# Two neighbouring banks per maximum instruction, and VectorE for seven of eight copies of the heads' bank

## The chip, the cores and the metric

The kernel runs on one core of a Trainium2 chip. The core has a matrix engine (TensorE, PE in the profile), a vector engine (VectorE, DVE), an activation engine (ScalarE, ACT), GpSimd (POOL) and a queue that issues DMAs (SyncE, SP). Matrix products land in PSUM, which the program treats as eight banks of 512 fp32 numbers in each of 128 partitions. The metric is the device time of one execution in microseconds. Before the change it is 3399.02 us, the median of three runs (3393.05 to 3400.91).

## The reference

For 16 batches of 1024 rows of 256 numbers:

```
x = x + layernorm(attention(layernorm(x)))     # on the left 128 columns, 16 heads of 8
x = x + layernorm(ffn(layernorm(x)))
attention: q, k, v = left @ W.T; softmax(q k^T / 4) over keys; out @ Wo.T + bo
ffn: 3 cycles of  h = gelu(h@w1+b1), gelu(h@w2+b2), gelu(h@w3+b3), sigmoid(h@w4+b4)
     out = out + coupling * twist(out)
```

The softmax needs, for each query row and head, the maximum over all 1024 keys. The kernel forms these maxima from products made for that purpose alone. They are subtracted inside the later score products, by three more rows of the queries (split in three bf16 parts), so that ScalarE's exponential needs no bias of its own.

## The kernel before

The program is written out engine by engine, each engine in its own loop over batches. Semaphores tie the engines together. A batch b passes an attention of 64 steps, and then a coupling of 30 beats, in which the network of batch b-1 runs beside the entry and exit work of other batches.

**A step of the attention.** One step handles four heads and one of eight blocks of keys. TensorE issues two score products (`scores`, line 499, first half), some maximum products (`max_unit`, line 481), two more score products, perhaps more maximum products, the weighing of the step before (`weigh`, line 514, eight passes in the trace), and a last maximum product. ScalarE does two exponentials over two banks each (`exp`, line 719). Eight steps make a group. At a group's end the bank `heads_ps` holds the weighted sums of four heads. ScalarE copies it to `headsT` (`take_heads`, line 728) after both exponentials of the next step, and the next group's first weighing waits for that copy through `heads_evac`.

**The maxima.** There are 256 units a batch. A unit is one product of 128 queries against 512 keys into one bank. VectorE reduces the bank to one column of `max_parts` (line 966). After 32 units a small VectorE instruction joins the two halves of the keys (`max_all`, line 972), GpSimd splits the result in three, and DMAs lay it as rows. Units of batch b+1 are worked on in the last part of batch b. In the attention of batch 0 a step has four units (1 after the first scores, 2 after the second scores, 1 after the weighing). In later attentions it has three (2, 0, 1).

**The ring.** `ring_bank` gives the bank whose last use is the oldest, and waits for the instruction that emptied it. In an attention there are three such banks, in a coupling five: the bank of the heads and one of the score banks join. Products other than maxima (transposes, projections) take banks of the same ring and count as two turns younger (`REST`). VectorE reads units strictly in their order, each as soon as `max_done` tells of it.

The number of units in a step or beat comes from these lines, and is not changed:

```python
return units_until(LEAD0 + 4 * n + (1, 3, 4)[third])                                # batch 0
return units_until(b * UNITS + LEAD + min(IN_ATTENTION, 3 * n + (2, 2, 3)[third]))  # later ones
```

The functions that the change touches follow.

Of the kernel before, what the change touches and what calls it, by code (L numbers as in the profile page):

```python
# [6 lines left out]
F32 = mybir.dt.float32  # L7
# [78 lines left out]
def attention_ffn_program(nc, a):  # L86
# [10 lines left out]
    with ExitStack() as ctx:  # L97
# [6 lines left out]
        scoresT_ps = ctx.enter_context(nc.psum_tensor("scoresT_ps", [P, 4 * BANK], F32))  # L104

        ring_ps = ctx.enter_context(nc.psum_tensor("ring_ps", [P, RING * BANK], F32))
        heads_ps = ctx.enter_context(nc.psum_tensor("heads_ps", [P, BANK], F32))
# [38 lines left out]
        max_parts = sb("max_parts", [P, 2, 2, MU])  # L146
# [100 lines left out]

        def laid(b):

            return 16 * (24 * (b // 2 + 1) - (12 if b % 2 == 0 else 0))  # L250
# [6 lines left out]
        banks = [ring_ps[:, i * BANK:(i + 1) * BANK] for i in range(RING)]  # L257
        banks += [scoresT_ps[:, FFN_BANKS * BANK:], heads_ps[:, :]]
# [3 lines left out]


# [4 lines left out]
        def layer_bank(b, l, second=0):  # L268
            i = FIRST_BANK[l] + second
            return banks[RING - 1 + i] if b == N - 1 else scoresT_ps[:, i * BANK:(i + 1) * BANK]  # L270

        def coupling_banks(l):
            i = FIRST_BANK[l]
# [172 lines left out]
        def tensor_program(e):  # L446
# [11 lines left out]
            def ring_bank(evacuated, count, rest=0):  # L458
                i = min(range(ring[0]), key=lambda k: turn[k])
# [15 lines left out]
            def max_unit(u):  # L475
# [5 lines left out]
                e.matmul(ring_bank(max_taken, u + 1),  # L481
# [3 lines left out]
            def scores(b, n, two):  # L485
# [11 lines left out]
                for side in range(2):  # L497
                    rows = slice(64 * side, 64 * side + ROWS + MROWS)
                    m = e.matmul(scoresT_ps[:, (2 - 2 * two + side) * BANK:(3 - 2 * two + side) * BANK],  # L499
# [212 lines left out]
        def scalar_program(e):  # L712
            def exp(b, n, two):
# [3 lines left out]
                if two == 0 and n == 0 and valid(b - 2):  # L717
                    e.wait_ge(ffn_done[0], BEATS * (b - 1))
                e.activation(p_sb[:, n % 2, 2 * two:2 * two + 2, :].rearrange("p h n -> p (h n)"),  # L719
                             scoresT_ps[:, (2 - 2 * two) * BANK:(4 - 2 * two) * BANK], ACT.Exp,  # L720
                             scale=SCALE).then_inc(exp_done, 1)

            def take_heads(b, n):
                group = n // NT
                e.wait_ge(pv_done, step_of(b, n) + 1)
# [167 lines left out]
            for b in range(-1, N):  # L893
                if b == 0:
                    e.wait_ge(const_dve, 2)
                for n in range(STEPS):
# [3 lines left out]
                    if valid(b) and n and n % NT == 0:  # L900
                        take_heads(b, n - 1)
                if valid(b):
                    take_heads(b, STEPS - 1)
# [49 lines left out]
        def vector_program(e):  # L953
            def max_units(done, upto):
                for u in range(done, upto):
                    if u < N * UNITS:
                        max_unit(u)
# [527 lines left out]
```

## Time and profile before

| | |
|---|---|
| median of three runs | 3399.02 us |
| all three | 3399.02, 3400.91, 3393.05 us |
| span of the profiled execution, first to last instruction | 3391.6 us |
| mean granted clock of TensorE | 0.985 of full |
| busy: TensorE, VectorE, ScalarE | 3222.9, 2992.7, 2843.6 us |
| TensorE waiting (weight loads) for VectorE's maxima, total over 2131 waits | 1242.4 us |
| maximum reductions on VectorE | 4096 of about 0.68 us |

The profiled execution's time with what lies outside the span is not recorded by itself. The span is 1.5 to 9.3 us below the three runs. In the profile PEld is the loading of weights, which overlaps the products, so that an idle time of PEld is not yet one of TensorE. The "idle before" of an engine names what ended the idle time.

### The profile page before, as it was taken

What the parts mean: (1) busy time and instruction counts of PE and PEld (TensorE: products, weight loads), DVE (VectorE), ACT (ScalarE), POOL (GpSimd) and SP (SyncE); (2) the same over time, 40 slices, a digit from 0 to 9 for tenths busy, and PEclk for the clock granted to TensorE, in tenths of its full rate; (3) what the DMA queues carried; (4) which work ended last, traced back from release to release, by engine and by line L of the source; (5) the groups of instructions that cost most, each with busy time, mean ns of one, the idle gap of its engine ahead of it and who ended that gap; (6) DMA issues with size and microseconds to landing.
All of it is one profiled execution on the core that took longest, in us unless ns stands there. A gap on an engine that the chain in (4) does not pass through costs nothing.

```text
span 3391.6 us, 56526 instructions
## 1 busy us (share of the span) xinstructions
PE 3222.9 (95%) x19712; PEld 941.5 (28%) x19712; DVE 2992.7 (88%) x5577; ACT 2843.6 (84%) x3752; POOL 897.6 (26%) x1322
## 2 busy tenths in 40 slices
PE   6989999999999999999999999999999999999987
PEld 2222232322323232232322323232232322323223
DVE  7999989999898998989989898998989989898943
ACT  3868979798897979979798897979979798896975
POOL 5002050321505123050320505123050320504015
PEclk7998999999999999999999999999999999999999
DMA  3111111121111112121121111112121121111001
GB/s 90 26 41 43 32 50 33 44 50 44 50 31 51 43 39 55 33 61 32 44 49 44 50 31 51 42 39 55 33 61 32 45 49 44 38 32 51 8 22 38
DMA packets 97498, 144.75 MB, mean 43 GB/s; under 512 B 49472, under 2 KB 60096, under 8 KB 89408
## 3 DMA queue, kind: packets, MB, share of 16 engines
q1 hardware_dynamic: 93520, 123.83, 13.8%
q0 software_dynamic: 3696, 17.31, 2.8%
q8 instruction: 158, 2.59, 0.3%
q14 instruction: 124, 1.02, 0.1%
HBM read 34.61 MB, written 32.51 MB: 20 GB/s over the span
## 4 chain that ended last, share of the span: by engine, by line
PE 67%; DVE 17%; ACT 8%; issue 3%; SPq 2%; DMA 1%; POOL 1%; DVEq 0%; POOLq 0%; ACTq 0%
PE heads_ps L514 24%; PE ring_ps L481 15%; DVE max_parts L966 12%; PE scoresT_ps L499 11%; PE scoresT_ps L602 7%; ACT p_sb L719 4%; DVE stats L977 3%; PE scoresT_ps L607 2%; ACT headsT L728 1%; PE ring_ps L543 1%; SPq L346 1%; DVE state L1030 1%; ACT state L784 1%; DVE moments L987 1%; PE ring_ps L529 1%
## 5 line engine op out<-in xcount | busy, mean ns | idle before, releaser
L966 DVE TENSOR_REDUCE max_parts<-ring_ps 128x1 f32<-128x512 f32 x3744 | 2369.2, 683 | 225.4 <-PE ring_ps L481 166.3
L719 ACT ACTIVATE p_sb<-scoresT_ps 128x1024 f32<-128x1024 f32 x2048 | 1970.1, 1024 | 81.4 <-PE scoresT_ps L499 57.7
L481 PE MATMUL ring_ps<-k_rows,q_rows 48*128 48x512 bf16 x3744 | 1086.0, 384 | 33.1 <-DVE max_parts L966 23.8
L514 PE MATMUL heads_ps<-p_sb,v_sb 128*9 128x512 f32 x8192 | 1071.4, 595 | 17.9 <-ACT headsT L728 11.9
L499 PE MATMUL scoresT_ps<-q_rows,k_rows 51*128 51x512 bf16 x4096 | 1021.3, 383 | 7.1 <-ACT p_sb L719 4.3
L481 PEld LDWEIGHTS ring_ps<-k_rows,q_rows 48*128 48x128 bf16 x3744 | 265.5, 94 | 1353.4 <-DVE max_parts L966 1242.4
L1233 POOL CAST max_wide<-max_all 128x16 bf16<-128x16 f32 x128 | 25.4, 198 | 1743.0 <-DVE max_all L972 1743.0
L602 PE MATMUL scoresT_ps<-state,w 128*128 128x512 f32 x732 | 364.9, 621 | 13.3 <-DVE state L1030 12.3
L824 ACT ACTIVATE p_sb<-scoresT_ps,b 128x512 f32<-128x512 f32 x180 | 123.8, 688 | 194.2 <-PE scoresT_ps L602 193.2
L499 PEld LDWEIGHTS scoresT_ps<-q_rows,k_rows 51*128 51x128 bf16 x4096 | 207.0, 93 | 224.4 <-ACT p_sb L719 211.5
L514 PEld LDWEIGHTS heads_ps<-p_sb,v_sb 128*9 128x9 f32 x8192 | 124.4, 88 | 288.8 <-issue 278.3
L607 PE MATMUL scoresT_ps<-p_sb,w 128*128 128x512 f32 x360 | 178.5, 618 | 0.1
L966 DVE TENSOR_REDUCE max_parts<-heads_ps 128x1 f32<-128x512 f32 x225 | 153.2, 681 | 24.0 <-PE heads_ps L481 23.2
L602 PEld LDWEIGHTS scoresT_ps<-state,w 128*128 128x128 f32 x732 | 125.6, 191 | 158.0 <-issue 151.4
L732 ACT ACTIVATE x_in<-x_in,offset,rstd 128x128 f32<-128x128 f32 (+1 forms) x248 | 119.9, 537 | 38.3 <-POOL offset L1243 38.3
L826 ACT ACTIVATE p_sb<-scoresT_ps,b 128x512 f32<-128x512 f32 x90 | 61.3, 681 | 76.8 <-PE scoresT_ps L607 76.8
L1241 POOL TENSOR_TENSOR rstd<-rstd,minus_half 128x8 f32<-128x8 f32 x63 | 111.3, 1767 | 5.2
L977 DVE BATCH_NORM_STATS2 stats<-x_in 128x6 f32<-128x256 f32 x248 | 90.9, 410 | 13.2 <-ACT x_in L792 9.8
L1240 POOL TENSOR_SCALAR rstd<-moments 128x8 f32<-128x8 f32 x63 | 15.9, 253 | 321.1 <-DVE moments L987 319.5
L1285 POOL TENSOR_TENSOR couple<-couple,state 128x512 f32<-128x512 f32 x60 | 76.5, 1275 | 71.8 <-ACT couple L815 71.8
L1294 POOL TENSOR_TENSOR state<-state,couple 128x512 f32<-128x512 f32 x60 | 77.8, 1297 | 64.8 <-DVE couple L1021 63.4
L966 DVE TENSOR_REDUCE max_parts<-scoresT_ps 128x1 f32<-128x512 f32 x127 | 86.2, 678 | 8.5 <-PE scoresT_ps L481 8.4
(196 smaller groups left out, 2635.9 us busy)
## 6 DMA issues: line engine op xcount, KB each, us to landing
q_rows<-parts SPq DMA_DIRECT2D x744, 32.0 KB
k_rows<-parts SPq DMA_DIRECT2D x744, 32.0 KB
x_sb<-in_x SPq DMA_DIRECT2D x16, 1024.0 KB, 4.8
x_in<-in_x SPq DMA_DIRECT2D x15, 1024.0 KB, 5.4
out<-x_sb SPq DMA_DIRECT2D x15, 1024.0 KB, 3.9
out<-x_in POOLq DMA_DIRECT2D x15, 1024.0 KB, 7.9
q_rows<-max_rows SPq DMA_DIRECT2D x512, 3.0 KB
feat_h<-headsT SPq DMA_DIRECT2D x512, 16.0 KB
```

What stands on the lines that cost most here:

```text
L481: e.matmul(ring_bank(max_taken, u + 1), q_rows[rows, slot, pair, h * BANK + qb * P:h * BANK + (qb + 1) * P], k_rows[rows, slot, pair, kh * ...
L499: m = e.matmul(scoresT_ps[:, (2 - 2 * two + side) * BANK:(3 - 2 * two + side) * BANK], k_rows[rows, slot, pair, kb * P:(kb + 1) * P], q_ro ...
L514: m = e.matmul(heads_ps[32 * j:32 * j + DH + 1, :], v_sb[:, b % 2, kb, 4 * (group % NG) + j, 0:DH + 1], p_sb[:, n % 2, j, :], start=(kb == ...
L602: o = e.matmul(ps, w1[:, f, m * P:(m + 1) * P], state[:, b % 2, f, c * BANK:(c + 1) * BANK], start=(f == 0), stop=(f == 1))
L607: o = e.matmul(ps, w2[:, f, :], hidden[k][:, 0, 2 * c + f, :], start=(f == 0), stop=(f == 1))
L719: e.activation(p_sb[:, n % 2, 2 * two:2 * two + 2, :].rearrange("p h n -> p (h n)"), scoresT_ps[:, (2 - 2 * two) * BANK:(4 - 2 * two) * BA ...
L732: m = e.activation(dst(t), src(t), ACT.Identity, bias=offset[i][:, t:t + 1], scale=rstd[i][:, t:t + 1])
L824: e.activation(hidden[k][:, 0, 2 * c + m, :], ps, ACT.Gelu, bias=b1[:, m:m + 1]).then_inc(hid_done[k], 1)
L966: e.tensor_reduce(max_parts[:, gi % 2, kh, col:col + 1], bank_of(max_taken, u + 1), AX.X, ALU.max).then_inc(max_taken, 1)
L977: m = e.bn_stats(stats[i][:, t, :], src(t))
L1241: finished(e.tensor_tensor(rstd[i][:, :], rstd[i][:, :], minus_half[:, :], ALU.pow))
L1294: e.tensor_tensor(half, half, couples[k][:, 2, :], ALU.add).then_inc(state_a_done[k], 1)
```

## The change

1. PSUM becomes one tensor, `all_ps`: banks 0 to 2 are the ring, 3 the heads, 4 to 7 the scores. The score banks swap their order, so that the one lent to the ring in a coupling (bank 4) lies beside the heads' bank. The coupling's layers keep to the other three.
2. TensorE's `max_units` looks, before each unit that is not the last of its stretch, for two neighbouring banks among the three oldest of the ring (`oldest_pair`). If there are two, this unit and the next take them, and VectorE reduces both with one instruction of 1024 elements that writes two columns. Both banks then wait for that one instruction to end. `max_parts` is laid out by unit, and the join reads it through a pattern.
3. VectorE copies the heads' bank in seven of eight groups (`take_heads`), between the second and the third stretch of units in the group's next step. ScalarE keeps the last copy of a batch, after its last exponential.

```diff
-                for u in range(done, upto):
-                    if u < N * UNITS:
-                        max_unit(u)
+                u, upto = done, min(upto, N * UNITS)
+                while u < upto:
+                    pair = oldest_pair() if u + 1 < upto else ()
+                    size = 2 if pair else 1
+                    first_of.append(u)
+                    for v in range(u, u + size):
+                        taken_by[v] = len(first_of)
+                        max_unit(v, pair[v - u:v - u + 1])
+                    u += size
+
+            def oldest_pair():
+                oldest = sorted(range(ring[0]), key=lambda k: turn[k])[:3]
+                pairs = [(i, j) for i, j in itertools.permutations(oldest, 2) if starts[j] - starts[i] == BANK]
+                return min(pairs, key=lambda ij: max(turn[ij[0]], turn[ij[1]])) if pairs else ()
...
-                e.tensor_reduce(max_parts[:, gi % 2, kh, col:col + 1], bank_of(max_taken, u + 1),
-                                AX.X, ALU.max).then_inc(max_taken, 1)
+                e.tensor_reduce(out, units_banks(u, size), AX.X, ALU.max).then_inc(max_taken, 1)
...
-                e.activation(headsT[:, group // NG, group % NG, :], heads_ps[:, :], ACT.Copy).then_inc(heads_evac, 1)
+                e.tensor_copy(headsT[:, group // NG, group % NG, :], heads_ps[:, :]).then_inc(heads_evac, 1)
...
                 for n in range(STEPS):
+                    upto = units_in_step(b, n, 1)
+                    max_units(done, upto)
+                    done = max(done, upto)
+                    if valid(b) and n and n % NT == 0:
+                        take_heads(b, n // NT - 1)
                     upto = units_in_step(b, n, 2)
```

In the whole program the order of VectorE after the change has 1393 reductions of two banks, 1310 of one, and 112 copies of the heads' bank. By place: 64 of two and 128 of one in the attention of batch 0, 64 and 64 in each later attention that has maxima throughout, about 24 and 15 in each full coupling.

VectorE in the attention of batch 0, before: units one by one, and a join after 32 of them.

```order
L966 TENSOR_REDUCE max_parts<-heads_ps 128x1
L966 TENSOR_REDUCE max_parts<-ring_ps 128x1 x6
L972 TENSOR_TENSOR max_all<-max_parts 128x16
L966 TENSOR_REDUCE max_parts<-ring_ps 128x1 x32
L972 TENSOR_TENSOR max_all<-max_parts 128x16
```

The same place after, across the end of a group of steps (128x2 is a reduction of two banks).

```order
L997 TENSOR_REDUCE max_parts<-all_ps 128x1 x2
L997 TENSOR_REDUCE max_parts<-all_ps 128x2
L1006 COPY headsT<-all_ps 128x512
L997 TENSOR_REDUCE max_parts<-all_ps 128x1
L1014 TENSOR_TENSOR max_all<-max_parts 128x16
L997 TENSOR_REDUCE max_parts<-all_ps 128x1
L997 TENSOR_REDUCE max_parts<-all_ps 128x2
```

Two of a step's four units share an instruction, and the copy stands between the shared one and the next single one.

ScalarE from the end of a coupling into the attention of batch 1, before.

```order
L771 ACTIVATE v_sb<-ring_ps 128x64x8
L784 ACTIVATE state,sums<-ring_ps 128x512
L719 ACTIVATE p_sb<-scoresT_ps 128x1024 x18
L728 ACTIVATE headsT<-heads_ps 128x512
L719 ACTIVATE p_sb<-scoresT_ps 128x1024 x16
```

And after.

```order
L801 ACTIVATE v_sb<-all_ps 128x64x8
L814 ACTIVATE state,sums<-all_ps 128x512
L749 ACTIVATE p_sb<-all_ps 128x1024 x128
L758 ACTIVATE headsT<-all_ps 128x512
L854 ACT_TABLE_LOAD
```

The 128 exponentials of a batch are no longer broken by copies, and the last copy stays where it was.

VectorE at the start of the attention of batch 1, before.

```order
L966 TENSOR_REDUCE max_parts<-scoresT_ps 128x1
L966 TENSOR_REDUCE max_parts<-ring_ps 128x1 x26
L972 TENSOR_TENSOR max_all<-max_parts 128x16
L966 TENSOR_REDUCE max_parts<-ring_ps 128x1 x32
L972 TENSOR_TENSOR max_all<-max_parts 128x16
```

And after, at the end of its first group of steps.

```order
L1014 TENSOR_TENSOR max_all<-max_parts 128x16
L997 TENSOR_REDUCE max_parts<-all_ps 128x1
L997 TENSOR_REDUCE max_parts<-all_ps 128x2
L997 TENSOR_REDUCE max_parts<-all_ps 128x1
L997 TENSOR_REDUCE max_parts<-all_ps 128x2
L1006 COPY headsT<-all_ps 128x512
L997 TENSOR_REDUCE max_parts<-all_ps 128x1
L997 TENSOR_REDUCE max_parts<-all_ps 128x2
```

A step of three units is now one reduction of two banks and one of one bank. TensorE's own order of products is the same as before.

## Rows read from the trace of the kernel before

**Rows 1.** The page: busy us (share of the span) and instructions of each engine.

```profile
PE 3222.9 (95%) x19712; PEld 941.5 (28%) x19712; DVE 2992.7 (88%) x5577; ACT 2843.6 (84%) x3752; POOL 897.6 (26%) x1322
```

**Rows 2.** Busy us by stretch: batch 0's attention and coupling, a later pair, its middle.

```profile
74.00:232.60 158.60, 148.86 (x1009) 33.37 (x1009) 156.26 (x260) 127.41 (x136) 7.91 (x34) 0.99 0.12 26
232.60:287.10 54.50, 39.11 (x128) 15.48 (x127) 47.36 (x110) 22.81 (x51) 23.12 (x32) 0.69 0.22 71
1508.30:1637.30 129.00, 127.43 (x949) 27.14 (x949) 121.03 (x199) 125.63 (x137) 12.90 (x31) 1.00 0.17 40
1637.30:1711.80 74.50, 70.50 (x283) 30.87 (x283) 63.71 (x148) 52.57 (x102) 41.99 (x50) 1.00 0.20 52
1657.40:1692.50 35.10, 31.98 (x121) 12.95 (x120) 34.27 (x90) 25.88 (x48) 24.12 (x28) 1.00 0.08 32
```

**Rows 3.** Timeline, ScalarE, a later attention: start us, us, engine, line, operation.

```profile
1590.71 0.60 ACT L728 ACTIVATE headsT<-heads_ps 128x512 f32<-128x512 f32 x1
...
1606.85 0.60 ACT L728 ACTIVATE headsT<-heads_ps 128x512 f32<-128x512 f32 x1
```

**Rows 4.** The chain that ended last, same place: start us, us, what.

```profile
1593.60 0.97 PE heads_ps L514 x8
...
1605.49 0.97 PE heads_ps L514 x8
```

**Rows 5.** Timeline, TensorE, one step of the same attention.

```profile
1602.43 0.39 PE L481 MATMUL ring_ps<-k_rows,q_rows 48*128 48x512 bf16 x1
...
1602.67 0.59 PE L481 MATMUL ring_ps<-k_rows,q_rows 48*128 48x512 bf16 x2
...
1603.05 0.10 PEld L499 LDWEIGHTS scoresT_ps<-q_rows,k_rows 51*128 51x128 bf16 x2 [0.17 <-ACT p_sb L719]
...
1604.38 0.39 PE L481 MATMUL ring_ps<-k_rows,q_rows 48*128 48x512 bf16 x1
...
1604.80 0.09 PEld L481 LDWEIGHTS ring_ps<-k_rows,q_rows 48*128 48x128 bf16 x1 [0.30 <-DVE max_parts L966]
```

**Rows 6.** Timeline, VectorE: durations and distances of its instructions.

```profile
1604.06 0.68 DVE L966 TENSOR_REDUCE max_parts<-ring_ps 128x1 f32<-128x512 f32 x1
...
1604.81 0.69 DVE L966 TENSOR_REDUCE max_parts<-ring_ps 128x1 f32<-128x512 f32 x1
...
1605.53 0.17 DVE L972 TENSOR_TENSOR max_all<-max_parts 128x16 f32<-128x16 f32 x1
...
1656.84 0.69 DVE L1059 TENSOR_TENSOR y_sb<-scoresT_ps,bo 128x512 f32<-128x512 f32 x1 [0.17 <-PE scoresT_ps L543]
1657.45 1.39 DVE L977 BATCH_NORM_STATS2 stats<-y_sb 128x6 f32<-128x256 f32 x4
...
1676.08 0.68 DVE L966 TENSOR_REDUCE max_parts<-scoresT_ps 128x1 f32<-128x512 f32 x1
1676.68 0.68 DVE L966 TENSOR_REDUCE max_parts<-ring_ps 128x1 f32<-128x512 f32 x1
```

**Rows 7.** Timeline, batch 0's attention: ScalarE over eight steps, then one step.

```profile
96.54 1.94 ACT L719 ACTIVATE p_sb<-scoresT_ps 128x1024 f32<-128x1024 f32 x2
...
116.41 1.94 ACT L719 ACTIVATE p_sb<-scoresT_ps 128x1024 f32<-128x1024 f32 x2
...
151.01 0.69 DVE L966 TENSOR_REDUCE max_parts<-ring_ps 128x1 f32<-128x512 f32 x1
...
151.75 0.39 PE L481 MATMUL ring_ps<-k_rows,q_rows 48*128 48x512 bf16 x1
...
153.05 0.39 PE L481 MATMUL ring_ps<-k_rows,q_rows 48*128 48x512 bf16 x1
...
153.47 0.69 DVE L966 TENSOR_REDUCE max_parts<-ring_ps 128x1 f32<-128x512 f32 x1
```

**Rows 8.** Timeline, first beat of a coupling: TensorE and ScalarE.

```profile
1641.78 0.39 PE L481 MATMUL ring_ps<-k_rows,q_rows 48*128 48x512 bf16 x1 [0.57 <-DVE max_parts L966]
...
1640.98 0.25 ACT L798 ACTIVATE hg<-ring_ps,gb 128x1 f32<-128x1 f32 x1
```

More of the change, by code:

```diff
@@ L246, in step_of, with pack_of @@
             return b * STEPS + n
+        first_of, taken_by = [], {}
+        def pack_of(u):
+            first = first_of[taken_by[u] - 1]
+            return first, 2 if taken_by.get(first + 1) == taken_by[u] else 1
         def laid(b):
@@ L256, in attention_ffn_program, with units_banks @@
         place = {}
-        banks = [ring_ps[:, i * BANK:(i + 1) * BANK] for i in range(RING)]
-        banks += [scoresT_ps[:, FFN_BANKS * BANK:], heads_ps[:, :]]
+        starts = [i * BANK for i in (*range(RING), RING + 1, RING)]
+        banks = [all_ps[:, at:at + BANK] for at in starts]
         def bank_of(evacuated, count):
             return banks[place[evacuated.name, count]]
+        def units_banks(u, size):
+            ends = [starts[unit_bank[v]] for v in (u, u + size - 1)]
+            both = all_ps[:, min(ends):max(ends) + BANK].rearrange("p (k n) -> p k n", n=BANK)
+            return both[:, ::-1, :] if ends[0] > ends[1] else both
+        unit_bank = {}
         def track(b):
@@ L269, in layer_bank @@
             i = FIRST_BANK[l] + second
-            return banks[RING - 1 + i] if b == N - 1 else scoresT_ps[:, i * BANK:(i + 1) * BANK]
+            if b == N - 1:
+                return banks[RING - 1 + i]
+            at = FFN_BANKS - FIRST_BANK[l] - (1 - second if LAYERS[l][0] == 4 else 0)
+            return scoresT_ps[:, at * BANK:(at + 1) * BANK]
         def coupling_banks(l):
-            i = FIRST_BANK[l]
+            i = FFN_BANKS - FIRST_BANK[l] - 1
             return scoresT_ps[:, i * BANK:(i + 2) * BANK].rearrange("p (s n) -> p s n", s=2)[:, :, 0:HALF]
@@ L456, in spare_banks, with ring_bank @@
                         turn[i], freed[i] = next(turns), last
-            def ring_bank(evacuated, count, rest=0):
-                i = min(range(ring[0]), key=lambda k: turn[k])
+            def ring_bank(evacuated, count, rest=0, i=None):
+                if i is None:
+                    i = min(range(ring[0]), key=lambda k: turn[k])
                 if freed[i]:
@@ L498, in scores @@
                     rows = slice(64 * side, 64 * side + ROWS + MROWS)
-                    m = e.matmul(scoresT_ps[:, (2 - 2 * two + side) * BANK:(3 - 2 * two + side) * BANK],
+                    m = e.matmul(scoresT_ps[:, (2 * two + side) * BANK:(2 * two + side + 1) * BANK],
                                  k_rows[rows, slot, pair, kb * P:(kb + 1) * P],
@@ L954, in max_units @@
             def max_units(done, upto):
[L955 to L973 removed]
+                u = done
@@ new lines, in max_units, with max_pack @@
+                while u < min(upto, N * UNITS):
+                    first, size = pack_of(u)
+                    max_pack(first, size)
+                    u = first + size
+            def max_pack(u, size):
+                for v in range(u, u + size):
+                    gi = v // PER_GROUP
+                    e.wait_ge(max_done[v % 2], v // 2 + 1)
+                    if v % PER_GROUP == 0 and gi >= 2:
+                        e.wait_ge(max_joined, gi - 1)
+                at, last = u % (2 * PER_GROUP), (u + size - 1) % (2 * PER_GROUP)
+                out = max_parts[:, last:at + 1][:, ::last - at] if last < at else max_parts[:, at:last + 1]
+                e.tensor_reduce(out, units_banks(u, size), AX.X, ALU.max).then_inc(max_taken, 1)
+                for v in range(u, u + size):
+                    if (v + 1) % PER_GROUP == 0:
+                        join(v // PER_GROUP)
```

53 lines of the change are left out of this document (27 added, 26 removed).

## The prediction, on record before the changed kernel ran

> **What bounds the kernel now.** I first read the busy shares [rows 1]: TensorE 95%, VectorE 88%, ScalarE 84%. No engine is simply full, so I went to the stretches [rows 2], which show four different limits.
>
> In a later attention (129.0 us, fifteen of them) TensorE is busy 127.4, ScalarE 125.6 and VectorE 121.0. The chain of waits has weighings from 1593.60 to 1605.49, six steps in 11.89 us, so a plain step takes 1.98 us [rows 4]. Two copies of the heads' bank by ScalarE are 16.14 us apart [rows 3]. Eight plain steps are 15.85, so a group's end costs 0.29. Within a step, TensorE's third score product waits for ScalarE's exponential [rows 5]. A maximum's weight load waits 0.30 for VectorE there, but the product itself follows the one before it at the array's own distance of 0.21 (two products of 0.38 in 0.59), so it would not start earlier without the wait. So the step is a loop between TensorE and ScalarE, and VectorE only fits in.
>
> In the attention of batch 0 (158.6 us) VectorE is busy 156.3. Eight steps take 19.87 us, 2.48 each [rows 7]. I can close the loop: a unit's reduction at 151.01 frees the bank of the unit whose product starts at 151.75 (0.74 later); the single unit behind the weighing starts at 153.05 (1.30 later); its reduction starts at 153.47 (0.42 later). Sum 2.46: that reuse is the step.
>
> In a later coupling (74.5 us) TensorE is busy 70.5, but its middle, 35.1 us long, has VectorE at 34.3 [rows 2]: there VectorE's throughput sets the pace. The coupling of batch 0 has VectorE at 47.4 of 54.5.
>
> **Prices.** Back to back, single reductions start 0.60 apart and last 0.68 [rows 6]. The reduction of two banks is not in the trace. Four BN_STATS of 256 elements last 1.39 together; each adds about 0.33, against 0.60 for 512, so 256 elements cost 0.27 and the second 512 about 0.54 (my estimate from these rows). I take 1.14 us from start to start and 1.22 duration. That saves 0.06 of a pair's 1.20. The ends: 1.20 (nothing saved) and 1.08 (twice the saving). VectorE's copy of 512 elements out of PSUM has its nearest row in the addition of the bias, 0.69 long and 0.61 to the next start [rows 6]; I take 0.60 and 0.68, with 0.48 and 0.69 as the ends. From a reduction's end to the weight load that it frees is 0.06 (1604.06 + 0.68 to 1604.80) [rows 5, 6].
>
> The Trainium skill ("VectorE: DVE Perf Modes", the section on the TRN2 errata) gives a VectorE instruction that reads PSUM 120 cycles plus one per element at 0.96 GHz. That would be 0.66 us for one bank, close to the 0.68 duration in [rows 6], and it would save 0.125 us for each pair rather than 0.06. The 0.60 from start to start speaks against the full 120 cycles, since part of them overlaps the next instruction. By the page the stretches where VectorE is full would gain twice as much (a rival below).
>
> **Batch 0's attention: pairs.** The ring has banks 0, 1, 2. A step takes a single unit, a pair, a single unit. Say a pair has 1 and 2. Then the singles take 0 and 1, and the next pair must be two neighbours of {2, 0, 1}: it becomes 0 and 1. Bank 1 is that of the unit just before. In the following step the singles take 2 and 0, and the pair 1 and 2, whose last user lies one unit further back. So in every second step, 32 times, TensorE's pair waits for the newest reduction. Its loop is the 2.46 from above plus the one single reduction between the two, 0.60: 3.06 us, against 2.46. The price of the pair's own reduction is not on that path. Cost 32 x 0.60 = +19.2 us. From the other side: it is 0 if something else covers it, but VectorE has no other work there.
>
> **Batch 0's attention: copies.** VectorE's copy starts after the pair's reduction, 0.42 + 1.14 = 1.56 after the pair's product; the single unit behind the weighing would start at 1.30 + 0.42 = 1.72; with the copy it starts at 2.16. Seven copies at 0.44: +3.1. ScalarE's copies cost nothing there: eight steps with one inside take 19.87 - 8 x 2.46 = 0.19 more, about the join of 0.17 [rows 6, 7]. Bounds 0 and 7 x 0.6 = 4.2.
>
> **Later attentions.** Three banks, and pair, single, pair, single always take (1,2), 0, (1,2), 0. Here VectorE's loop runs: single product to its reduction 0.43 (1604.38 to 1604.81), to the pair's 0.60, until both banks are free 1.22 + 0.06, and from the second product of a pair (1602.88, as the x2 row ends at 1603.26) to the next single product 1.50 (1604.38) [rows 5, 6]. Sum 3.81 for two steps, against 3.96. It fits with 0.15 to spare, so the plain step stays 1.98. At a group's end the copy enters: 0.43 + 0.60 + 1.14 (pair, then copy) + 0.60 (copy) + 0.60 (single) + 1.28 (pair freed) + 1.50 = 6.15 for three steps of 5.94. So the copy on VectorE costs 0.20, where ScalarE's costs 0.29. What goes on ScalarE comes back, for the most part, as a late release of the pair. Gain 0.09 x 7 x 15 = -9.5. The weighing of the new group needs the copy by about 2.97 after that single product and has it at 2.17 + 0.68 + 0.06 = 2.91, just in time. Two of six joins in an attention stand behind a single unit, and their 0.17 or a little more uses up the 0.15: I put 0.05 on each, +1.5. Together -8.0. The ends: -30.5 if the copy is free (0.29 x 105), and +6 if the copy is 0.1 longer in effect and joins cost their full 0.17.
>
> **Couplings.** In the middle of each of 14 full couplings are 9 or 10 pairs: -0.6. In the first beat five units come at once while a small product holds one of five banks. Before, the fifth unit waited 0.57 for a reduction, until 1641.78. Now the pair search leaves it the bank that ScalarE frees at 1640.98 + 0.25, so that it can go about 0.45 earlier [rows 8]: -0.45. Against that, a pair chosen for being neighbours is less old than the oldest: about five packs in a coupling take a bank of the pack just before them. Each could cost up to 0.5 (release 0.06, product 0.39, its signal 0.04) if VectorE had nothing in between; mostly it has statistics or an update there. I take +0.4 together, between 0 and 2.5. Net -0.65 x 14 = -9. The two couplings before batch 1's attention have 48 pairs, mostly where VectorE is full: -2.
>
> **Sum.** +19.2 + 3.1 - 8.0 - 9 - 2 = +3.3 us. Against the profiled span that is 3391.6 + 3.3 = 3394.9, and with the same distance to the median as before, 3399.0 + 3.3 = 3402. VectorE's busy time falls by about 1393 x 0.14 (two durations of 0.68 become one of 1.22) and rises by 112 x 0.68: 2992.7 - 195 + 76 = about 2875. ScalarE's falls by 112 x 0.60 = 67.
>
> **Rivals.**
> - *The copy leaves ScalarE for nothing* (faster). For it: VectorE has 8 us idle in a later attention, and 0.15 to spare per two steps. It decides if a pair's banks are free earlier than I think, or the copy is 0.48. Then -30.5 in the attentions, no stalls in the couplings (-15), -3 in the first ones, with batch 0's +22: -26. Time 3373.
> - *A pair's late release stalls TensorE in the couplings* (slower). For it: TensorE works in order, and its layer products stand behind the waiting unit. Against: in the middle VectorE is behind anyway. It decides from about three fully exposed stalls in a coupling. With four, +2.0 - 1.05 = +0.95 each, x 14 = +13, and 22.3 - 8.0 - 2 for the rest: +25. Time 3424.
> - *Batch 0's pair wait is hidden*: without the +19.2, 3383.
> - *The fixed part of an instruction is saved in full*: another 0.06 on some 135 pairs in the couplings and 48 before: -11. Time 3391. The page cited above is the rule behind it.
>
> **Chances.** Forecast 0.40, with its own range 3391 to 3413; copy for nothing 0.24; stalls 0.22; hidden wait 0.08; full saving 0.06. A difference under 0.2% (6.8 us) can't be told from none. The forecast's case gives 0.05 faster, 0.22 same, 0.13 slower; the stalls are all slower; the copy for nothing and the hidden wait are faster but for 0.01; the last is split 0.04 and 0.02. Faster 0.40, same 0.25, slower 0.35. The range runs from 3373, where the copy costs nothing, to 3428, a little past four stalls a coupling.
>
> **What would show it.** Batch 0's attention 181 us long rather than 158.6, with steps alternating between about 3.1 and 2.5. Later attentions at 128.5, each group's end near 0.2 long, the plain step still 1.98. The pair's reduction near 1.22. Couplings at 73.9. If batch 0's attention is not longer, the ring argument is wrong. If the plain step moves, VectorE's loop was not the loose one. If couplings are longer than 74.5, the stalls are real.

## The result and the profile after

The changed kernel takes 3442.8 us (median of four runs, 3439.8 to 3446.0). The kernel before takes 3398.6 in the same comparison. The ratio is 1.0135, with a 95% interval of 1.012 to 1.0149: slower by 44 us, where 3 were forecast and 3428 was the upper end. One run of a later version (no pairs in the last three beats of a coupling) took 5073 us at a mean granted clock of 0.554 and is left out of its figures.

The page after shows the engine shares, the chain by engine, and the group of the maximum reductions. These answer to [rows 1].

```profile
PE 3229.5 (94%) x19712; PEld 933.8 (27%) x19712; DVE 2981.0 (87%) x4296; ACT 2809.0 (82%) x3640; POOL 893.3 (26%) x1322
...
PE 58%; DVE 26%; issue 6%; SPq 5%; ACT 2%; DMA 2%; POOL 1%; DVEq 0%; POOLq 0%
...
L997 DVE TENSOR_REDUCE max_parts<-all_ps 128x2 f32<-128x1024 f32 (+1 forms) x2703 | 2492.9, 959 | 322.7 <-PE all_ps L511 277.1
```

VectorE is busy 12 us less, yet its share of the chain that ended last rose from 17% to 26%. It has less to do and is waited for more (the chain before, on its page):

```profile
PE 67%; DVE 17%; ACT 8%; issue 3%; SPq 2%; DMA 1%; POOL 1%; DVEq 0%; POOLq 0%; ACTq 0%
```

Next, the groups of VectorE with shapes kept apart (count, then busy us and mean ns of one, then the idle time before them).

```profile
L997 DVE TENSOR_REDUCE max_parts<-all_ps 128x2 f32<-128x1024 f32 x1393 | 1687.1, 1215 | 131.4 <-PE all_ps L511 128.4 <-issue 1.2
L997 DVE TENSOR_REDUCE max_parts<-all_ps 128x1 f32<-128x512 f32 x1310 | 893.6, 687 | 191.3 <-PE all_ps L511 148.6 <-DVE max_all L1014 0.5
...
L1006 DVE COPY headsT<-all_ps 128x512 f32<-128x512 f32 x112 | 76.2, 681 | 15.2 <-PE all_ps L544 15.2
```

The prices were right: the pair lasts 1.215 us (1.22 forecast), the copy 0.681 (0.68).

The stretches after, in the order of [rows 2]: the attention of batch 0, the coupling behind it, a later attention, a later coupling. The columns are start:end and length, then busy time (and count) of PE, PEld, DVE, ACT, POOL, then the granted clock, DMA share and GB/s.

```profile
77.00:262.10 185.10, 167.96 (x1007) 31.57 (x1008) 161.88 (x205) 123.84 (x129) 7.82 (x34) 0.95 0.10 23
262.10:322.10 60.00, 40.55 (x135) 16.40 (x127) 46.94 (x90) 23.43 (x50) 23.06 (x32) 0.61 0.22 68
1552.20:1681.00 128.80, 126.78 (x949) 26.30 (x946) 120.91 (x142) 123.38 (x130) 12.17 (x31) 1.00 0.16 38
1681.00:1756.80 75.80, 70.32 (x283) 31.17 (x285) 62.65 (x123) 52.45 (x100) 41.94 (x50) 1.00 0.20 53
```

VectorE had 2.3 us idle in batch 0's attention before, and has 23 now.

I divided both profiled executions at ScalarE's exponentials, and set the differences of all stretches against the forecast's terms. An attention reaches from the first start to the last end of its 128 exponentials, and a coupling fills the time between two attentions. The differences add up to the 51.1 us between the two spans. That is 7 more than between the medians: the span before lies only 1.5 us under the fastest of its four runs. So some microseconds of the table may be spread between executions.

| part | forecast | measured |
|---|---|---|
| prologue | (in -2) | +3.0 |
| batch 0's attention | +22.3 | +26.5 |
| coupling before batch 1 | -2 | +5.6 |
| attention of batch 1 | (in -8.0) | +2.4 |
| 14 later couplings | -9 | +17.0 |
| 14 later attentions | -8.0 | -3.7 |
| tail | 0 | +0.4 |

Two rows are far off: the couplings by 26 us, and the early stretches around the first coupling by 13.

**The clock.** The granted clock in the early stretches was this in the kernel before:

```profile
237.50:278.40 40.90, 28.21 (x71) 11.13 (x71) 35.38 (x87) 14.29 (x29) 18.15 (x28) 0.58 0.20 66
```

And after:

```profile
268.40:278.60 10.20, 3.62 (x8) 2.52 (x8) 7.93 (x18) 1.85 (x5) 3.47 (x8) 0.50 0.55 160
285.50:329.90 44.40, 35.87 (x113) 12.37 (x117) 32.72 (x57) 23.94 (x45) 19.59 (x24) 0.50 0.17 56
```

Of the 40.9 us before, 34.2 are at half (1.2 GHz of 2.4). After there are 54.6, and the last 8 of them lie in the attention of batch 1, where TensorE sets the pace. The forecast had no term for the clock in these stretches.

In batch 0's attention the clock also dips, which means here that it is granted at half for some 3.4 us and then at full again. The first row is a whole group of eight steps, from one copy of the heads' bank to the next, with such a dip in it (the third row). The second is a group without. The fourth is the dip in the last group.

```profile
102.05:126.08 24.03, 21.94 (x131) 4.08 (x128) 20.66 (x28) 15.50 (x16) 0.83 (x4) 0.93 0.10 22
172.90:195.75 22.85, 20.61 (x131) 3.84 (x128) 20.61 (x28) 15.50 (x16) 0.83 (x4) 1.00 0.11 24
104.60:108.00 3.40, 3.40 (x16) 0.58 (x16) 2.25 (x3) 0.60 (x1) 0.07 (x1) 0.50 0.16 34
...
244.60:248.00 3.40, 3.40 (x20) 0.76 (x16) 2.72 (x4) 1.73 (x2) 0.00 (x0) 0.51 0.18 39
```

A dip of 3.4 us costs that group 1.18 us. Three groups have one (the second, the third and the last), and in the first group the clock is at half for 6.8 us.

**The couplings.** At the end of a later coupling TensorE projects the values into a bank of the ring, and works in order. Before (start us, us, engine, line; in brackets the idle time before it, shown where it is large):

```profile
1708.50 1.29 DVE L966 TENSOR_REDUCE max_parts<-ring_ps 128x1 f32<-128x512 f32 x2 [0.38 <-PE ring_ps L481]
...
1709.25 0.60 PE L535 MATMUL ring_ps<-wv,feat_x 128*128 128x128 f32 x3
```

After, the same place:

```profile
1753.58 1.82 DVE L997 TENSOR_REDUCE max_parts<-all_ps 128x2 f32<-128x1024 f32 x2 [0.58 <-PE all_ps L511]
...
1754.86 0.60 PE L565 MATMUL all_ps<-wv,feat_x 128*128 128x128 f32 x3 [0.77 <-DVE max_parts L997]
```

Before, the projection starts 0.75 us after the first of two reductions began: that one lasts 0.69, and the release takes 0.06. After, it starts 1.28 after the pair's reduction began: 1.22 and 0.06. It wanted one bank and had to wait for two.

The projection isn't the only place. I compared the two kernels product by product in the coupling behind batch 12's attention (three other couplings give the same figures within 0.03). The columns are the time into the coupling before, TensorE's wait there before and after, and how far the changed kernel is behind once that place is passed.

| place | product | wait before | wait after | behind |
|---|---|---|---|---|
| 4.5 | fifth maximum of the first beat | 0.57 | 0.08 | -0.48 |
| 21.7 | a maximum | 0.00 | 0.67 | -0.05 |
| 27.1 | a maximum | 0.00 | 0.27 | +0.22 |
| 38.8 | a maximum | 0.18 | 0.51 | +0.55, back to +0.34 by 60 |
| 62.6 | a maximum | 0.00 | 0.56 | +0.89 |
| 71.9 | projection of the values | 0.13 | 0.77 | +1.67, and +1.34 at the end |

The place at 62.6, before:

```profile
2717.38 0.38 PE L481 MATMUL heads_ps<-k_rows,q_rows 48*128 48x512 bf16 x1
```

And after:

```profile
2768.19 0.39 PE L511 MATMUL all_ps<-k_rows,q_rows 48*128 48x512 bf16 x2 [0.56 <-DVE max_parts L997]
```

So about half a microsecond of a coupling's loss arises at a maximum, and 0.44 of the projection's 0.64 reaches the end.

### The profile page after: what moved, and what is told of

It is laid out like the page before. It is cut to its first block, busy times and chain, and to the rows that moved or that the text cites. A ratio compares the mean times of both kernels' runs of the same rounds, so it can differ in the third digit from the quotient of the medians.

```text
span 3442.7 us, 56452 instructions
## 1 busy us (share of the span) xinstructions
PE 3229.5 (94%) x19712; PEld 933.8 (27%) x19712; DVE 2981.0 (87%) x4296; ACT 2809.0 (82%) x3640; POOL 893.3 (26%) x1322
## 4 chain that ended last, share of the span: by engine, by line
PE 58%; DVE 26%; issue 6%; SPq 5%; ACT 2%; DMA 2%; POOL 1%; DVEq 0%; POOLq 0%
DVE max_parts L997 19%; PE all_ps L544 19%; PE all_ps L511 14%; PE all_ps L529 8%; PE all_ps L632 7%; SPq L362 3%; PE all_ps L637 3%; DVE stats L1019 3%; PE all_ps L573 2%; DVE headsT L1006 2%; SPq L337 1%; PE all_ps L559 1%; ACT p_sb L749 1%; PE all_ps L565 1%; DMA max_rows<-max_wide 1%
## 5 line engine op out<-in xcount | busy, mean ns | idle before, releaser
L997 DVE TENSOR_REDUCE max_parts<-all_ps 128x2 f32<-128x1024 f32 (+1 forms) x2703 | 2492.9, 959 | 322.7 <-PE all_ps L511 277.1
L749 ACT ACTIVATE p_sb<-all_ps 128x1024 f32<-128x1024 f32 x2048 | 1974.2, 1021 | 144.8 <-PE all_ps L529 105.1
L511 PE MATMUL all_ps<-k_rows,q_rows 48*128 48x512 bf16 x4096 | 1108.8, 391 | 104.0 <-DVE max_parts L997 82.3
L544 PE MATMUL all_ps<-p_sb,v_sb 128*9 128x512 f32 x8192 | 1074.8, 597 | 7.3 <-ACT p_sb L749 4.9
L529 PE MATMUL all_ps<-q_rows,k_rows 51*128 51x512 bf16 x4096 | 1032.5, 384 | 3.4 <-ACT p_sb L749 2.3
L511 PEld LDWEIGHTS all_ps<-k_rows,q_rows 48*128 48x128 bf16 x4096 | 256.9, 93 | 1503.2 <-DVE max_parts L997 1242.0
L632 PE MATMUL all_ps<-state,w 128*128 128x512 f32 x768 | 382.6, 622 | 8.4 <-DVE state L1072 6.0
L854 ACT ACTIVATE p_sb<-all_ps,b 128x512 f32<-128x512 f32 x180 | 123.7, 687 | 193.0 <-PE all_ps L632 192.5
L529 PEld LDWEIGHTS all_ps<-q_rows,k_rows 51*128 51x128 bf16 x4096 | 208.4, 93 | 199.8 <-ACT p_sb L749 188.4
L637 PE MATMUL all_ps<-p_sb,w 128*128 128x512 f32 x360 | 178.5, 618 | 0.1
L856 ACT ACTIVATE p_sb<-all_ps,b 128x512 f32<-128x512 f32 x90 | 61.3, 681 | 79.7 <-PE all_ps L637 79.7
L1341 POOL TENSOR_TENSOR state<-state,couple 128x512 f32<-128x512 f32 x60 | 77.6, 1294 | 54.5 <-DVE couple L1063 53.1
L1006 DVE COPY headsT<-all_ps 128x512 f32<-128x512 f32 x112 | 76.2, 681 | 15.2 <-PE all_ps L544 15.2
```

The costliest lines, as they stand in the source:

```text
L511: e.matmul(ps, q_rows[rows, slot, pair, h * BANK + qb * P:h * BANK + (qb + 1) * P], k_rows[rows, slot, pair, kh * BANK:(kh + 1) * BANK], s ...
L529: m = e.matmul(scoresT_ps[:, (2 * two + side) * BANK:(2 * two + side + 1) * BANK], k_rows[rows, slot, pair, kb * P:(kb + 1) * P], q_rows[r ...
L544: m = e.matmul(heads_ps[32 * j:32 * j + DH + 1, :], v_sb[:, b % 2, kb, 4 * (group % NG) + j, 0:DH + 1], p_sb[:, n % 2, j, :], start=(kb == ...
L632: o = e.matmul(ps, w1[:, f, m * P:(m + 1) * P], state[:, b % 2, f, c * BANK:(c + 1) * BANK], start=(f == 0), stop=(f == 1))
L637: o = e.matmul(ps, w2[:, f, :], hidden[k][:, 0, 2 * c + f, :], start=(f == 0), stop=(f == 1))
L854: e.activation(hidden[k][:, 0, 2 * c + m, :], ps, ACT.Gelu, bias=b1[:, m:m + 1]).then_inc(hid_done[k], 1)
```

## The experiments

### Pairs taken out, copies kept

```diff
-                    pair = oldest_pair() if u + 1 < upto else ()
+                    pair = oldest_pair() if u + 1 < upto and False else ()
```

> The changed kernel with every maximum reduced by itself and banks taken oldest first; VectorE still makes the copies. Ring theory (a pair takes a bank whose last reader stands just ahead, and frees both late): batch 0's attention falls from 185.2 to about 161 (158.6 plus a little for seven copies on VectorE), the couplings from 75.8 to 74.5, later attentions 129.2, since single reductions leave VectorE less room for the copy; time about 3400. Rival (the copies on VectorE are what costs): batch 0's attention stays above 170 and the time above 3425.

Measured: 3410.1 us, ratio 1.0032 (1.0023 to 1.0042). Its stretches, batch 0's attention and a later coupling:

```profile
74.60:237.30 162.70, 149.16 (x1009) 33.30 (x1009) 159.90 (x267) 123.87 (x129) 7.90 (x34) 0.99 0.11 26
1849.80:1924.30 74.50, 70.56 (x283) 30.88 (x283) 63.95 (x148) 52.62 (x102) 42.02 (x50) 1.00 0.20 52
```

The full couplings are those of before, so all of their loss comes from the pairs. A later attention takes 129.62: without pairs VectorE's copies cost 0.6 each attention, and 4.1 in batch 0.

### Copies back on ScalarE, pairs kept

```diff
-                    if valid(b) and n and n % NT == 0:
-                        take_heads(b, n // NT - 1)
```

This goes from VectorE's loop, and the lines removed from ScalarE's come back.

> The changed kernel with all copies of the heads' bank back on ScalarE; pairs as changed. Ring theory: batch 0's attention about 182 (3 us less), couplings unchanged at 75.8, later attentions about 129.0 (0.2 more); time about 3443, the same as the changed kernel. Rival (copies on VectorE cost): time below 3425.

Measured: 3446.4 us, ratio 1.0132 (1.0114 to 1.015). Batch 0's attention:

```profile
75.60:253.10 177.50, 163.48 (x1008) 30.70 (x1008) 158.21 (x198) 127.42 (x136) 7.87 (x34) 0.99 0.11 24
```

Pairs alone cost 18.9 us there, against the 19.2 forecast. A group of eight steps is 22.35 long (copies by ScalarE on the chain of time, two of them):

```profile
144.39 0.60 ACT L758 ACTIVATE headsT<-all_ps 128x512 f32<-128x512 f32 x1
166.74 0.60 ACT L758 ACTIVATE headsT<-all_ps 128x512 f32<-128x512 f32 x1
```

With VectorE's copy and a full clock it is 22.85 (above). So the copy costs 0.50 each, 3.5 for seven, near the forecast's 0.44 and 3.1. The other 4.2 us of the difference of 7.7 go with the clock. The changed kernel has four dips of 3.4 us more in this stretch (one in each of three groups, and 6.8 rather than 3.4 us in its first group), and 4 x 1.18 = 4.7.

### Batch 0 one by one

```diff
+                    pair = oldest_pair() if u + 1 < upto and stage != ["step", 0] else ()
```

`stage` holds the kind of stretch, its batch, and where needed the number of the step or beat that TensorE's program is written for.

> The changed kernel with no pairs in the attention of batch 0 alone. Ring theory: that attention falls by about 23 us to 162, nothing else moves by more than 1 us: time about 3420. Rival (VectorE as such is too full there, whoever is paired): falls by less than 5 us.

Measured: 3417.4 us, ratio 1.0051 (1.0036 to 1.0066). Batch 0's attention is 162.4. The coupling behind it also fell, from 60.0 to 55.2, though the pairs in it are unchanged. The coupling has 30.7 us at half clock and the attention behind it 3.4, together as much as before. This looks as if the slow attention had passed the loss on, but the next experiment speaks against so simple an account.

### Pairs in the later attentions only

```diff
+                    pair = oldest_pair() if u + 1 < upto and stage[0] == "step" and stage[1] > 0 else ()
```

> The changed kernel with pairs only in the attentions of batches 1 to 15, none in batch 0's attention or in any coupling. Ring theory: batch 0's attention 162, couplings 74.4 each (0.4 less if the wait in their first beat goes by the new order of banks, as there it did with pairs), first couplings back at 74.0 and 54.4, later attentions 128.8: time about 3392, near the kernel before or a little under it. Rival (the couplings lose by the new layout or by what VectorE leaves over from the attention): couplings stay at 75.8 and the time at about 3412.

Measured: 3406.3 us, ratio 1.0022 (1.001 to 1.0033). The couplings are back at 74.47, as expected, but not the time. Five attentions in a row (batches 5 to 9) took 130.2 to 130.6 rather than 128.7, each with a dip of the clock. The last experiment below turns on them.

Batch 0's attention is 162.4, and neither it nor the coupling behind it has a pair. Even so that coupling is not back at 54.5:

```profile
237.40:295.10 57.70, 42.72 (x127) 16.60 (x126) 47.70 (x110) 23.21 (x50) 23.20 (x32) 0.63 0.22 71
```

It has 43.2 us at half clock, and 8.0 follow in the attention of batch 1. Over the profiled executions this coupling goes with its time at half clock, whatever the pairs: 53.1 us with 27.3 at half (no pairs), 54.4 with 34.1 (before), 57.7 with 43.2 (here), 60.0 with 46.9 (changed). What keeps the clock at half for so long is not shown.

### The same banks, read one by one

This tells apart what the choice of the banks costs and what the common instruction costs. Each bank has an instruction of its own, the choice is that of the change.

```diff
-                    first_of.append(u)
                     for v in range(u, u + size):
+                        first_of.append(v)
                         taken_by[v] = len(first_of)
```

> The banks are chosen exactly as in the changed kernel, neighbours among the three oldest, but each bank is reduced and given back by an instruction of its own. Theory 1 (one instruction for two banks needs both products and returns both banks together, so that VectorE idles while TensorE fills them): without it VectorE is busy through, batch 0's attention falls back from 185.2 us to about 162.7 (the 162.7 without pairs), full couplings from 75.8 to 74.5, the whole to about 3411. Theory 2 (taking a bank that is not the oldest costs by itself): the banks are the same, so batch 0's attention stays over 175 us and couplings near 75.5, the whole about 3435.

Measured: 3457.4 us, ratio 1.0171 (1.0158 to 1.0184). Batch 0's attention, and a later coupling (five are like it; six have a dip of the clock and take 76.2 to 77.0; one takes 75.7 without one):

```profile
77.00:262.60 185.60, 158.66 (x1008) 33.28 (x1008) 161.97 (x268) 123.81 (x128) 7.75 (x33) 0.95 0.10 22
862.60:937.20 74.60, 71.02 (x286) 31.16 (x286) 63.65 (x149) 52.69 (x103) 41.92 (x50) 1.00 0.20 52
```

Each theory is right in one place. In batch 0 the choice alone does all the damage (185.6, my expectation of 162.7 fell). In the couplings without a dip the choice costs 0.1 and the common instruction the other 1.2: product by product, the maximum at 62.6 and the projection lose nothing here. The whole is still slower than the changed kernel. The later attentions take 129.6 rather than 128.8, and ten dips stand in couplings and attentions where the changed kernel has none. Two steps of batch 0 in this run, TensorE:

```profile
152.86 0.39 PE L511 MATMUL all_ps<-k_rows,q_rows 48*128 48x512 bf16 x1
...
154.04 0.39 PE L511 MATMUL all_ps<-k_rows,q_rows 48*128 48x512 bf16 x1 [0.35 <-DVE max_parts L997]
154.63 0.39 PE L511 MATMUL all_ps<-k_rows,q_rows 48*128 48x512 bf16 x1 [0.21 <-DVE max_parts L997]
...
155.93 0.39 PE L511 MATMUL all_ps<-k_rows,q_rows 48*128 48x512 bf16 x1
...
158.40 0.39 PE L511 MATMUL all_ps<-k_rows,q_rows 48*128 48x512 bf16 x1
```

And VectorE:

```profile
153.29 2.49 DVE L997 TENSOR_REDUCE max_parts<-all_ps 128x1 f32<-128x512 f32 x4 [0.37 <-PE all_ps L511]
156.35 2.48 DVE L997 TENSOR_REDUCE max_parts<-all_ps 128x1 f32<-128x512 f32 x4 [0.58 <-PE all_ps L511]
```

The steps are 3.07 and 2.47 long, the forecast's 3.06 and 2.46. In the long one TensorE's second and third maxima wait for reductions of the step itself, the weighing stands behind them, and VectorE then has 0.58 with nothing to read. With three banks, one reused a place too early is enough.

### Pairs only where the two oldest banks are neighbours

```diff
-                oldest = sorted(range(ring[0]), key=lambda k: turn[k])[:3]
+                oldest = sorted(range(ring[0]), key=lambda k: turn[k])[:2]
```

> A pair is formed only where the two oldest banks are neighbours: 155 pairs in the full couplings rather than 337, of which 16 (before 71) take a bank of the pack just before them; 43 rather than 64 pairs in batch 0's attention, none but one with the newest bank; the later attentions keep theirs. Theory 1a (what costs is a pair on a bank of the pack just before): batch 0's attention about 163 us, full couplings about 74.7, the whole about 3400 to 3405. Theory 1b (each pair costs by its joint release, however old its banks are): batch 0's attention about 175 (43/64 of the extra), couplings about 75.1, the whole about 3425.

Measured: 3424.2 us, ratio 1.0072 (1.0059 to 1.0085). Batch 0's attention and a later coupling, then the projection of the values in it.

```profile
74.70:237.00 162.30, 151.87 (x1009) 29.72 (x1009) 160.31 (x226) 123.87 (x129) 7.81 (x34) 0.99 0.12 26
1654.90:1730.40 75.50, 70.11 (x283) 30.79 (x283) 63.23 (x138) 53.13 (x102) 42.20 (x50) 1.00 0.20 53
```

And TensorE's row:

```profile
1728.19 0.49 PE L565 MATMUL all_ps<-wv,feat_x 128*128 128x128 f32 x2 [0.87 <-DVE max_parts L997]
```

Again one theory holds in each place. In batch 0 the 43 pairs with the oldest banks cost nothing. In the couplings 155 pairs rather than 337, and 16 rather than 71 that take a bank of the instruction just before, still cost 1.08 of the 1.34 us. So neither how young a pair's banks are nor how many pairs there are explains the loss. It comes in the same two places as in the changed kernel: product by product, a coupling is 0.13 behind until the maximum at 62.6, 0.67 after it, and then the projection waits 0.74 us longer than before.

### No pairs in the last three beats of a coupling

```diff
+                    pair = oldest_pair() if u + 1 < upto and not (
+                        stage[0] == "beat" and stage[1] > 0 and stage[2] >= BEATS - 3) else ()
```

> As the changed kernel, but no pair in the last three beats of the full couplings. In the changed kernel's trace the projection of the values takes a bank of the pair just before it and waits 0.77 us for its one instruction, where before it waited 0.13 for the first of two. Theory (TensorE's other products wait for the joint release): the wait is back at 0.13 and full couplings fall from 75.8 to 75.15, the whole to about 3434. Rival (the loss is spread, and a later wait takes its place): couplings within 0.2 of 75.8, the whole about 3442.

Measured: 3440.1 us (three runs), ratio 1.0129 (1.0111 to 1.0147). A coupling, and then TensorE's row of the projection in another:

```profile
2086.50:2161.80 75.30, 70.49 (x283) 31.06 (x283) 63.30 (x126) 52.63 (x102) 41.95 (x50) 1.00 0.20 52
```

```profile
1749.72 0.49 PE L566 MATMUL all_ps<-wv,feat_x 128*128 128x128 f32 x2
```

The wait of 0.77 is gone (0.14 is left), and the coupling is 0.44 shorter, of the 0.64 expected. The maximum at 62.6 still waits 0.56. The whole time can't be told from the changed kernel's: 1.0129 against 1.0135, with intervals that overlap. Five attentions now have a dip of the clock that the changed kernel did not have (1.6 to 1.9 us each), and they give back the 5 us won.

### Pairs in the attentions and in the first beat

```diff
+                    pair = oldest_pair() if u + 1 < upto and (
+                        stage[1] > 0 and (stage[0] == "step" or stage[2] == 0)) else ()
```

> Pairs in the attentions of batches 1 to 15 and in the first beat of the couplings only (five units at once), nowhere in batch 0. As forecast: the first beat's gain of 0.45 is kept, full couplings 74.0. Rival (the middle, where VectorE is full, swallows it, since VectorE's work is the same): 74.4 to 74.5 as with no pairs. Batch 0's attention 162.4 either way, the whole 3398 to 3408.

Measured: 3415.1 us, ratio 1.0059 (1.0038 to 1.008). Both expectations missed: couplings of 75.1, and five of them with a dip take 76.7 to 77.0. The first beat's fifth unit:

```profile
1852.59 0.61 PE L512 MATMUL all_ps<-k_rows,q_rows 48*128 48x512 bf16 x4
1854.40 0.39 PE L512 MATMUL all_ps<-k_rows,q_rows 48*128 48x512 bf16 x1 [1.20 <-DVE max_parts L1000]
```

Here the ring comes into the coupling in another order, the fifth unit gets a bank of a pair, and waits 1.20, where it waited 0.57 before and 0.08 in the changed kernel. The gain that I had forecast for this beat hangs on which bank comes up, not on the pair search as such.

### Layout alone

Every maximum by itself and all copies on ScalarE, on the new places of the banks and with the new `max_parts` (both edits above together).

> The new places of the banks and the new max_parts alone: every maximum by an instruction of its own, all copies on ScalarE. If layout and join cost nothing: 3398, batch 0's attention 158.6, later attentions 129.0, couplings 74.45. The difference to the version with single maxima and VectorE's copies (162.7 and 129.6) is then the copies' own price without pairs: 4.1 in batch 0 and 0.6 for each later attention. Rival: the join through a pattern costs some 0.1 us more each, 0.6 for each attention; then 3406 and the copies are free.

Measured: 3398.9 us, ratio 1.0000 (0.9991 to 1.0009), later attentions 129.07, couplings 74.47. The layout and the join's pattern cost nothing that can be told from none. The prologue has 47.8 us at half clock here as in the changed kernel (37.5 before) and is 75.1 long rather than 74.0, so about 1 of the 3.0 us in the table needs no pair.

### Each stage as it does best, and the start of an attention

Pairs in the later attentions only, copies by ScalarE in batch 0 and by VectorE later:

```diff
-                    if valid(b) and n and n % NT == 0:
+                    if valid(b) and b and n and n % NT == 0:
                         take_heads(b, n // NT - 1)
```

ScalarE's own copy stands where it stood before, for batch 0 alone.

> Pairs only in the attentions of batches 1 to 15, copies by VectorE there, by ScalarE in batch 0; couplings and batch 0 one by one. From the phases of the earlier runs: batch 0's attention 158.6 as before, couplings 74.5, later attentions 128.8: 15 x 0.25 = 3.8 gained. If the granted clock stays full in the attentions of batches 5 to 9, about 3394; if it halves for some us at the start of each of them as in the run with the same pairs (five times 1.5 us), about 3402. A rival: the changed order of the banks in the prologue costs by itself, then above 3402.

Measured: 3404.5 us (3394.6 to 3415.0, twelve runs), ratio 1.0016 (1.0005 to 1.0027). Then the same with pairs from the third step on:

```diff
+                    pair = oldest_pair() if u + 1 < upto and (
+                        stage[0] == "step" and stage[1] > 0 and stage[2] >= 2) else ()
```

> As the version with pairs in the later attentions only and ScalarE's copies in batch 0, but pairs begin with the third step of each attention. In that version TensorE waited 0.88 us in the first three of an attention and the granted clock then fell to half for 3.4 us in eight of fifteen attentions, 1.6 us longer each. Theory (these waits bring the clock down): without them no such stretches, later attentions 128.7, the whole about 3394. Rival (the clock falls for another reason, such as the whole attention's pattern): some attentions still 130.2, the whole 3400 to 3405.

Measured: 3390.5 us (3387.2 to 3393.0), ratio 0.9979 (0.9969 to 0.9988), faster than both kernels. TensorE at the start of an attention in the first of the two:

```profile
1512.74 0.39 PE L512 MATMUL all_ps<-k_rows,q_rows 48*128 48x512 bf16 x1 [0.18 <-ACT state L822]
...
1513.66 0.39 PE L530 MATMUL all_ps<-q_rows,k_rows 51*128 51x512 bf16 x2 [0.22 <-ACT p_sb L752]
1514.52 0.39 PE L512 MATMUL all_ps<-k_rows,q_rows 48*128 48x512 bf16 x2 [0.47 <-DVE max_parts L1007]
```

The stretches that follow:

```profile
1512.60:1514.80 2.20, 1.36 (x10) 0.45 (x10) 1.77 (x3) 2.20 (x4) 2.20 (x3) 1.00 0.37 75
1514.80:1518.20 3.40, 3.40 (x18) 0.56 (x15) 1.98 (x3) 1.67 (x3) 3.24 (x4) 0.51 0.77 248
1518.20:1530.00 11.80, 11.80 (x91) 2.43 (x88) 10.74 (x14) 11.39 (x12) 3.17 (x6) 1.00 0.16 49
```

With pairs from the third step:

```profile
1505.90:1508.20 2.30, 1.86 (x11) 0.59 (x10) 2.30 (x5) 2.30 (x5) 2.30 (x3) 1.00 0.57 116
1508.20:1511.60 3.40, 3.40 (x29) 0.70 (x28) 2.79 (x4) 3.24 (x4) 3.24 (x4) 1.00 0.72 239
1505.90:1634.40 128.50, 127.24 (x950) 26.60 (x949) 120.81 (x144) 123.36 (x130) 12.93 (x31) 1.00 0.17 40
```

The first version idles TensorE for 0.84 of 2.20 us, and does 18 products in the next 3.4 us, against 29. Eight of fifteen of its attentions (batches 7 to 14) have such a dip, the second version's one. A dip costs 1.6 us, and an attention without one is 128.66 in the first, 128.48 in the second. The first version's runs range over 20 us (with mean granted clocks from 0.974 to 0.981) and the second's over 6. So leaving the pairs out of the first two steps takes most of the dips away, and this is shown. That the length of the waits decides is not. The same three waits stand at the start of this version's attentions of batches 3 to 6, which have no dip, and of twelve attentions of the version with pairs in the first beat, of which one has a dip. And in the changed kernel TensorE idles for longer there, 1.26 us in one piece in the attentions of batches 2 to 14, and the clock stays full in all of them:

```profile
1553.76 0.39 PE L511 MATMUL all_ps<-k_rows,q_rows 48*128 48x512 bf16 x1 [1.26 <-DVE max_parts L997]
```

```profile
1552.20:1554.50 2.30, 1.04 (x10) 0.33 (x7) 1.82 (x3) 2.00 (x5) 2.22 (x4) 1.00 0.37 53
1554.50:1557.90 3.40, 3.40 (x28) 0.65 (x26) 3.28 (x4) 3.40 (x4) 3.32 (x3) 1.00 0.75 302
```

## Why the prediction was wrong

The step that failed is the stalls in the couplings, "+0.4 together, between 0 and 2.5". Three mistakes lie in it. I counted the pairs with young banks and priced those, but with hardly any of them left a coupling still loses 1.08. I looked only for maxima that wait, and TensorE's other products want a pair's banks too: the projection of the values waits 0.64 longer, of which 0.44 reaches the coupling's end. And I took most of the waits to be covered by VectorE's other work, while one maximum alone (at 62.6) costs half a microsecond. The gain of 0.45 set against them did come (a wait of 0.08 in place of 0.57), yet it was lost again after 22 of the 75 us, at a maximum that now waits 0.67. Net +1.2 a coupling (+1.34 in a plain one) in place of -0.65. The rival of stalls in the couplings was the right mechanism. Its own price of 3424 was short by 4 us in the couplings and mainly by the early stretches, which it had at -2 too.

The other terms, in order:

- *Batch 0's pairs, +19.2.* Right: 18.9, with steps of 3.07 and 2.47. The reason given, the choice of banks and not the common instruction, is shown by the same banks read one by one.
- *Batch 0's copies, +3.1.* 3.5 for the copies; the dips of the clock add some 4 that no term had.
- *The first two couplings, -2.* Wrong in sign: +3.0 and +5.6, and +2.4 more in the attention of batch 1. The first goes with 10 us more at half clock, the other two with about 20. With batch 0 one by one 4.8 of the 5.6 are gone, but with single maxima in the couplings as well 3.3 of them are back, so their cause stays open.
- *Later attentions, -8.0.* -0.25 each in the changed kernel, 3.7 in all. A group of eight steps with VectorE's copy takes 16.03 us in place of 16.14, 0.11 less where 0.09 was forecast, and two of seven take 16.27. The table shows why the two edits belong together there (an attention in us, full clock):

| | one by one | pairs |
|---|---|---|
| copies by ScalarE | 129.07 | 129.05 |
| copies by VectorE | 129.62 | 128.77 |
| the same, no pairs in the couplings | | 128.66 |
| the same, pairs from the third step | | 128.48 |

  Neither edit gains alone. Together they gain 0.3, and 0.55 where the couplings and the first two steps are left as they were: 15 x 0.55 = 8.2, near the forecast's 8.0. What I missed is the start of the attention, where the ring comes over from the coupling: TensorE waits there 1.26 us in one piece in the changed kernel, 0.43 in all before.
- *Prices.* From a pair's start to the next reduction's is 1.14 us (the row at 1753.58: 1.82 for both, less 0.68), as estimated. A pair saves 0.06 of 1.20. The rival of the full saving (0.12) has nothing for it.
- *VectorE busy 2875.* 2981. I subtracted durations (0.14 a pair), but a stretch counts overlapping instructions once, so that a pair saves 0.06 and a copy adds 0.60: 2992.7 - 84 + 67 = 2976.

The range failed with the stalls and the early stretches. Its upper end allowed four stalls of 0.5 us and nothing for the clock.

## What to carry to other kernels

An instruction that empties two buffers gives both back at its own end. Price it not by what it saves its engine but by everyone who wants either buffer next, users of another kind than those that it serves included. In a short ring, taking another buffer than the oldest can be a cost by itself (23 us in batch 0's attention with three banks, 0.1 us in a coupling with five), so compare the order of release, not the count of instructions. When an edit adds waits of some tenths of a microsecond to TensorE, read the granted clock of what comes next before the sum is believed. And an edit may be right in one stage and wrong in the others: tried stage by stage it gained 0.2% here, where it lost 1.35% as a whole.

## What the runs showed of the hardware

In eight of fifteen attentions the granted clock fell to half for 3.4 us after TensorE had been idle for 0.84 us in 2.20, in three waits of which the longest was 0.47. After the same waits it stayed full in others, and also after 1.26 us of idle time in one piece. In such a dip TensorE did 18 products, against 29 in 3.4 us at full clock. A dip cost 1.2 us in batch 0's attention and 1.6 to 1.9 us in a later one.

A reduction out of PSUM of 1024 elements takes 1215 ns, one of 512 elements 687: 528 ns for 512 more, and some 160 ns that don't depend on the size. The Trainium skill ("VectorE: DVE Perf Modes", the section on the TRN2 errata) has 120 cycles and one per element at 0.96 GHz, 1.19 and 0.66 us, and these durations agree within 5%. From start to start 0.60 and 1.14 us are nearly in proportion, though, so that most of the fixed part overlaps the next instruction, and joining two saves little.
